# Sums over states turned from channel-by-token to token-by-channel in a bidirectional state-space layer

## The reference, cut to what matters

```
xz = x @ W_in.T
xp, z = split(xz, 2)
xc = silu(conv4(xp) + conv_b)                       # causal, per channel
dt, Bt, Ct = split(xc @ W_xproj.T)
dt = softplus(dt @ W_dt.T + b_dt)
h[t] = exp(dt[t] * A) * h[t-1] + (dt[t] * xc[t]) * Bt[t]    # 16 states per channel
y[t] = sum over states of h[t] * Ct[t]
y = (y + xc * D_param) * silu(z)
out = y @ W_out.T
...
return 0.5 * (mamba(x) + flip(mamba(flip(x))))      # forwards and backwards in time
```

## Time and profile before

| what | value |
|---|---|
| time, median of 3 runs | 4728.89 us (4722.57 to 4737.03) |
| span of the profiled execution, first to last instruction | 4718.1 us |
| POOL busy over the span | 3212.3 us (68%) |
| DVE busy | 3251.1 us (69%) |
| PE busy | 4271.6 us (91%) |
| ACT busy | 2430.7 us (52%) |

### The profile page before, as it was taken

How to read it: one execution, slowest core, us unless ns; L and a number is a source line. 1 busy time by engine, 2 the same in 40 slices (tenths; PEclk the granted TensorE clock), 3 DMA queues, 4 the chain that set the end, 5 groups by cost and what they waited for, 6 DMA issues and landing times. The chain is left out here.

```text
span 4718.1 us, 62490 instructions
## 1 busy us (share of the span) xinstructions
PE 4271.6 (91%) x16896; PEld 2235.4 (47%) x16896; DVE 3251.1 (69%) x5016; ACT 2430.7 (52%) x4880; POOL 3212.3 (68%) x1669
## 2 busy tenths in 40 slices
PE   7999986997899999999999999999999876999994
PEld 4666644664343443344334434433443334666673
DVE  5667773111699999999999999989999975111114
ACT  3555542122566666767676666667666633222221
POOL 3222222442799999999999999999999941444441
PEclk9999996998899999999999999999999987999997
DMA  1000011342334333334333333333333321333456
GB/s 35 21 20 20 20 53 59 108 127 76 107 114 125 115 118 116 121 109 121 122 112 115 112 121 118 116 118 113 117 107 123 114 67 45 110 116 112 127 169 219
DMA packets 267113, 478.79 MB, mean 101 GB/s; under 512 B 39404, under 2 KB 176444, under 8 KB 266908
## 3 DMA queue, kind: packets, MB, share of 16 engines
q1 hardware_dynamic: 235776, 403.02, 26.9%
q0 software_dynamic: 28032, 73.17, 6.1%
q10 hardware_dynamic: 3100, 0.64, 0.1%
HBM read 409.75 MB, written 41.81 MB: 96 GB/s over the span
## 5 line engine op out<-in xcount | busy, mean ns | idle before, releaser
L1804 POOL TENSOR_TENSOR m_xh<-m_u,m_Bb 128x1536 f32<-128x1536 f32 x512 | 1780.1, 3550 | 51.6 <-DVE m_u L1675 39.0
L1731 PE MATMUL bank<-m_xh,ident 128*128 128x512 f32 x3072 | 1455.1, 609 | 34.3 <-POOL m_xh L1793 34.3
L1773 DVE TENSOR_TENSOR_SCAN bank<-bank,m_xh 128x512 f32<-128x512 f32 x864 | 1038.9, 1216 | 44.5 <-ACT bank L1760 42.2
L1760 ACT ACTIVATE bank<-m_dt,m_Ac 128x508 f32<-128x508 f32 x1536 | 1024.9, 683 | 38.4 <-DVE m_xh L1773 38.4
L1731 PEld LDWEIGHTS bank<-m_xh,ident 128*128 128x128 f32 x3072 | 576.2, 194 | 820.0 <-issue 730.7
L1773 DVE TENSOR_TENSOR_SCAN m_xh<-bank,m_xh 128x512 f32<-128x512 f32 x672 | 787.8, 1207 | 64.8 <-ACT bank L1760 59.3
L1793 POOL TENSOR_TENSOR m_xh<-m_xh,m_Cb 128x1536 f32<-128x1536 f32 x224 | 794.0, 3544 | 4.3 <-DVE m_xh L1773 4.0
L1784 DVE TENSOR_TENSOR m_xh<-bank,m_Cb 128x512 f32<-128x512 f32 x864 | 581.3, 673 | 10.9 <-DMA m_Cb<-BC_rows 10.8
L1204 ACT ACTIVATE f1t_h<-bank,f1t_b 128x512 f32<-128x512 f32 (+1 forms) x276 | 147.6, 586 | 509.9 <-PE bank L1234 509.9
L1134 POOL DMA_INDIRECT rows_y<-f1t_y,f1t_home x142 | 139.9, 985 | 316.4 <-DVE f1t_y L1175 287.1
L1579 PE MATMUL bank<-m_xp,m_dg 128*128 128x512 f32 x768 | 351.9, 601 | 3.7 <-DVE m_u L1675 1.4
(11 more groups left out here) (367 smaller groups left out, 6148.3 us busy)
## 6 DMA issues: line engine op xcount, KB each, us to landing
m_Bb<-BC_rows SPq DMA_DIRECT2D x256, 512.0 KB, 4.8
m_Cb<-BC_rows SPq DMA_DIRECT2D x256, 512.0 KB, 4.0
f1t_w<-f_w SPq DMA_DIRECT2D x46, 576.0 KB
m_r<-m_dt POOLq DMA_DIRECT2D x32, 768.0 KB, 7.4
f1t_w1a<-f_w SPq DMA_DIRECT2D x46, 384.0 KB
f0t_w<-f_w SPq DMA_DIRECT2D x22, 576.0 KB
f1c_yg<-rows_y SPq DMA_DIRECT2D x16, 768.0 KB, 8.3
f1t_w1b<-f_w SPq DMA_DIRECT2D x92, 96.0 KB
```

What stands on the lines that cost most here:

```text
L1731: mm = pe.matmul(bank[:, c, :], K.ident[:, :], xh[n % NX][:, c, :], start=False, stop=(d == 1 and n == NS - 1))
L1760: act.activation(o[:, :, lo:hi], seqs(dt[d][:, c, :])[:, :, lo:hi], ACT.Exp, scale=Ac[:, c, n:n + 1]).then_inc(s_dA, 1)
L1773: dve.tensor_tensor_scan(o, bank[:, RING[d][p], way], xh[n % NX][:, c, way], 0.0, ALU.mult, ALU.add).then_inc(s_h, 1)
L1804: pool.tensor_tensor(xh[n % NX][:, :, :], u[d][:, :, :], Bb[q % RB][:, n % QN, :].unsqueeze(1).to_broadcast([P, DC, TOK]), ALU.mult).then_ ...
```

## The change

The sums are kept with tokens on partitions and channels along the free axis. `pe_sum` makes four fp32 transposes of 128 x 128 (one per sequence) that add into PSUM, in place of one product with the identity of 128 x 512. `pe_D` makes four products of 128 columns per block. The gate is computed with tokens on partitions too: four products of 384 columns (`pe_gate`), four copies (`act_gate`). `dve_y` becomes four multiplications of 128 x 384, and each needs all three blocks' sums. Since W_out still wants channels on partitions, the gated rows are turned back: for each block c four transposes on PE (`pe_yT`) into bank `NB` and a copy by ACT (`act_ys`) into `lw`, which `pe_out` then reads. The D terms of a group now all follow the last `dve_y` of the group before, at units 13 to 15; a sum may catch up three units at a time instead of two. `pe_out` moves from units 17 and 18 to 18 and 20, `dve_out` from 14 and 15 to 16 and 17, `pe_dt1` from 20 to 22 up to 22 to 24.

```diff
-            "y": (6, 7, 9), "pe_D0": (14, 15, 17), "pe_D1": (6, 16, 25), "pe_out": (17, 18), "out": (14, 15),
+            "y": (6, 7, 8, 9), "pe_D0": (13, 14, 15), "pe_D1": (6, 16, 25), "pe_yT": (15, 16, 17), "act_ys": (15, 16, 17),
+            "pe_out": (18, 20), "out": (16, 17),
...
-        ys = r
+        ysT = r.rearrange("p c t -> p (c t)").rearrange("p (s x) -> p s x", s=G)
...
-        gz = sb("gz", [P, DC, TOK])
+        ys = lw
+        gz = sb("gz", [P, G, DC * P])
+        yb = bank[:, 0:DC, :].rearrange("p b x -> p (b x)")
...
-                m = slice((DC + c) * P, (DC + c + 1) * P)
-                pe.matmul(bank[:, front(c), :], win_a[:, m], zTa[:, :], start=True, stop=False)
-                pe.matmul(bank[:, front(c), :], win_b[:, m], zTb, start=False, stop=True).then_inc(s_zps, 1)
+                m, t = slice(DC * P, 2 * DC * P), slice(c * P, (c + 1) * P)
+                pe.matmul(bank[:, NB, 0:DC * P], zTa[:, t], win_a[:, m], start=True, stop=False)
+                pe.matmul(bank[:, NB, 0:DC * P], zTb[:, t], win_b[:, m], start=False, stop=True).then_inc(s_zps, 1)
...
         def pe_D(pe, g, d, c):
             pe.wait_ge(s_xc, g * 2 + d + 1)
-            if d == 0 and later(g):
-                pe.wait_ge(s_gy, (g - 1) * DC + c + 1)
+            if d == 0 and c == 0 and later(g):
+                pe.wait_ge(s_gy, g * G)
...
-            pe.matmul(bank[:, c, :], dgD[:, c, :], xc[d][:, c, :], start=(d == 0), stop=False).then_inc(s_D, 1)
+            for i in range(G):
+                b = i * DC + c
+                mm = pe.matmul(yb[:, b * P:(b + 1) * P], xc[d][:, c, i * P:(i + 1) * P], dgD[:, c, :],
+                               start=(d == 0 and c == 0 and i != 1), stop=False, skip_group_check=True)
+            mm.then_inc(s_D, 1)
...
-            mm = pe.matmul(bank[:, c, :], K.ident[:, :], xh[n % NX][:, c, :], start=False, stop=(d == 1 and n == NS - 1))
+            for i in range(G):
+                b = i * DC + c
+                mm = pe.matmul(yb[:, b * P:(b + 1) * P], xh[n % NX][:, c, i * P:(i + 1) * P], K.ident[:, :], is_transpose=True,
+                               start=False, stop=(d == 1 and n == NS - 1), skip_group_check=True)
             mm.then_inc(s_red, 1)
+
+        def pe_yT(pe, g, c):
+            if c == 0:
+                pe.wait_ge(s_gy, g * G + G)
+                if not (isinstance(g, int) and g == NG - 1):
+                    pe.wait_ge(s_pj, g * 2 + 4)
+                    stand_alone(pe, K.go)
+            else:
+                pe.wait_ge(s_ys, g * DC + c)
+            for i in range(G):
+                mm = pe.transpose(bank[:, NB, i * P:(i + 1) * P], ysT[:, i, c * P:(c + 1) * P], K.ident[:, :])
+            mm.then_inc(s_ysps, 1)
+
+        def act_ys(act, g, c):
+            act.wait_ge(s_ysps, g * DC + c + 1)
+            if c == 0:
+                act.wait_ge(s_spps, (g + 1) * 2 * DC + (DC if not (isinstance(g, int) and g == NG - 1) else 0))
+            act.copy(ys[:, c, :], bank[:, NB, :]).then_inc(s_ys, 1)
 
         def pe_out(pe, g, i):
             if i == 0:
-                pe.wait_ge(s_gy, g * DC + DC)
-                if not (isinstance(g, int) and g == NG - 1):
-                    pe.wait_ge(s_pj, g * 2 + 4)
+                pe.wait_ge(s_ys, g * DC + DC)
...
-        def dve_y(dve, g, c):
-            dve.wait_ge(s_red, (g * 2 * NS + 2 * NS - 1) * DC + c + 1)
-            if c == 0:
+        def dve_y(dve, g, i):
+            if i == 0:
+                dve.wait_ge(s_red, (g + 1) * 2 * NS * DC)
                 dve.wait_ge(s_gz, g + 1)
-            dve.tensor_tensor(ys[:, c, :], bank[:, c, :], gz[:, c, :], ALU.mult).then_inc(s_gy, 1)
+            dve.tensor_tensor(ysT[:, i, :], yb[:, i * DC * P:(i + 1) * DC * P], gz[:, i, :], ALU.mult).then_inc(s_gy, 1)
...
-                now = list(range(done, min(upto, done + 2)))
+                now = list(range(done, min(upto, done + 3)))
```

More of the change, by code:

```diff
@@ L1434, in mamba_phase @@
         s_er, = ctx.software(K, 1)
-        s_gy, s_ops, s_out = sem("gated_ready"), sem("outps_ready"), sem("res_ready")
+        s_gy, s_ysps, s_ys = sem("gated_ready"), sem("gated_back"), sem("gated_copied")
+        s_ops, s_out = sem("outps_ready"), sem("res_ready")
         def seqs(t):
@@ L1558, in pe_gate @@
                 else:
-                    pe.wait_ge(s_zc, g * DC + c)
-                m = slice((DC + c) * P, (DC + c + 1) * P)
-                pe.matmul(bank[:, front(c), :], win_a[:, m], zTa[:, :], start=True, stop=False)
-                pe.matmul(bank[:, front(c), :], win_b[:, m], zTb, start=False, stop=True).then_inc(s_zps, 1)
+                    pe.wait_ge(s_zc, g * G + c)
+                m, t = slice(DC * P, 2 * DC * P), slice(c * P, (c + 1) * P)
+                pe.matmul(bank[:, NB, 0:DC * P], zTa[:, t], win_a[:, m], start=True, stop=False)
+                pe.matmul(bank[:, NB, 0:DC * P], zTb[:, t], win_b[:, m], start=False, stop=True).then_inc(s_zps, 1)
             def act_gate(act, c):
-                act.wait_ge(s_zps, g * DC + c + 1)
+                act.wait_ge(s_zps, g * G + c + 1)
                 if c == 0 and deep:
-                    act.wait_ge(s_gy, g * DC)
-                act.copy(gz[:, c, :], bank[:, front(c), :]).then_inc(s_zc, 1)
+                    act.wait_ge(s_gy, g * G)
+                act.copy(gz[:, c, :], bank[:, NB, 0:DC * P]).then_inc(s_zc, 1)
             def pe_conv(pe, c):
@@ L1643, in act_ln @@
                     act.wait_ge(s_spps, s * DC)
+                if d == 1 and deep:
+                    act.wait_ge(s_ops, g * 2)
                 act.activation(lw[:, :, :], w1[d][:, :, :], ACT.Ln).then_inc(s_ln, 1)
@@ L1656, in pe_sp @@
                     if d == 1:
-                        pe.wait_ge(s_zc, g * DC + DC)
+                        pe.wait_ge(s_zc, g * G + G)
                         stand_alone(pe, K.go)
@@ L1695, in chain @@
                     continue
-                for c in range(DC):
+                for c in range(G if name == "gate" else DC):
                     put("pe", POS[f"pe_{name}{d}"][c], on_pe, c)
@@ L1719, in pe_D @@
             pe.wait_ge(s_xc, g * 2 + d + 1)
-            if d == 0 and later(g):
-                pe.wait_ge(s_gy, (g - 1) * DC + c + 1)
-            elif d == 0:
+            if d == 0 and c == 0 and later(g):
+                pe.wait_ge(s_gy, g * G)
+            elif d == 0 and c == 0:
                 pe.wait_ge(s_u, DC)
-            pe.matmul(bank[:, c, :], dgD[:, c, :], xc[d][:, c, :], start=(d == 0), stop=False).then_inc(s_D, 1)
+            for i in range(G):
[3 more added lines that the diff above has]
+            mm.then_inc(s_D, 1)
         def pe_sum(pe, g, d, n, c):
@@ L1855, in sums_at @@
                 upto = p + 1 - LAG * DC
-                begun = sum(p >= at for at in POS["pe_D0"])
-                if carry and begun < DC:
-                    upto = min(upto, begun)
-                now = list(range(done, min(upto, done + 2)))
+                if carry and p < POS["pe_D0"][-1]:
+                    upto = min(upto, 0)
+                now = list(range(done, min(upto, done + 3)))
                 plan.append(now)
@@ L1909, in main @@
                             pe_sum(pe, *at_step(g, d, k // DC), k % DC)
+                    if carry and p in POS["pe_yT"]:
+                        pe_yT(pe, g - 1, POS["pe_yT"].index(p))
                     if carry and p in POS["pe_out"]:
@@ L1916, in after @@
                             pe_sum(pe, NG - 1, 1, n, c)
+                    for c in range(DC):
+                        pe_yT(pe, NG - 1, c)
                     for i in two:
@@ L1924, in main, with after @@
                     act_decay(act, g, d, p)
-                program(act, "act", main, lambda act: None, lambda act: None)
+                    if d == 0 and later(g) and p in POS["act_ys"]:
+                        act_ys(act, g - 1, POS["act_ys"].index(p))
+                def after(act):
+                    for c in range(DC):
+                        act_ys(act, NG - 1, c)
+                program(act, "act", main, lambda act: None, after)
             @block.gpsimd
@@ L1956, in after @@
                     dve_read(dve, NG - 1, 1, UNITS - 1)
-                    for c in range(DC):
-                        dve_y(dve, NG - 1, c)
+                    for i in range(G):
+                        dve_y(dve, NG - 1, i)
                     for i in two:
```

8 lines of the change are left out of this document (4 added, 4 removed), and 4 rows, old and new, of the table POS.

## The result

The changed kernel takes 4899.36 us, median of 4 runs (4897.85 to 4906.4), the kernel before 4728.53 beside it: a ratio of 1.0367 (95% interval 1.035 to 1.0383). It is slower by 171 us, outside the range of the prediction. The profiled execution has a span of 4896.1 us.

A forecast was written before the change was run, and what follows sets the result against it. POOL was taken to bound the state-space layer (159.94 of 162.96 us a group). Terms -29 + 20 + 2 = -7 us on a span of 4718.1 gave about 4711, a 4722 us median (own range 4708 to 4738); overall range 4700 to 4762.

The forecast's parts named there:

- the 36.3 us: POOL's waits in the layer for u inside the loop, sum slots and DVE's scans: all a faster PE can win.
- PE's freed 38 us a group: PE time saved by shorter sums, taken to cover the extra D and gate products, which were costed at nothing.
- The slower rival: Clock falls ahead of the second convolution block as PE idles; gate 2.4 us later, +36, 4758 us; chance 0.18.
- one sign that the text gave: Clock at 0.50 around the second convolution block, with scan waits at state 3, would show the clock was the cause.
- The rule that spoke against it: Skill page: transposes don't count as busy TensorE, so sums as transposes would not hold the clock; 4758 us by it.
- The new wait: DVE waits 2.9 and 1.1 us at the output additions; POOL feels 1.3 us a group, +20 us.
- the faster rival: The turning back is hidden, POOL feels 0.3 us a group: -26, 4703 us; chance 0.28.
- The 1.0 us gained at the gate: DVE's wait for sums at the first gate multiplication, 1.95 us, gets 1.0 us shorter, between 0 and 1.6.
- The gain of 29 us: Shorter sums cut POOL's waits: 16 us for u, 10 for slots, 3 for scans; bounds -36 and -12.
- Sums: A sum on PE becomes four fp32 transposes, 0.46 us in place of 0.855, saving 38 us a group.
- an accumulating transpose costs a product's time: Rival: sums stay at 0.855 us, nothing of the gain is won, the new wait stays: +22, 4751 us; chance 0.09.
- The end: After the last sum nothing hides the turn: gate to first output 7.9 us, today 4.7; +2 us in all.

The follow-up runs named there:

- e9_fill_first: The changed kernel with products of zeros filling TensorE's waits in the chain of a group's first half alone, none for the second half: 4751.1 us.
- e1_plain: The changed kernel with its sums as ordinary fp32 products by the identity instead of transposes, all else as changed: 5048.4 us.
- e4_before_late: The kernel before with only the changed kernel's later positions for output, dt products, gate and softplus steps; sums and layout as before: 4800.1 us.
- e11_noturn_fill: The changed kernel with waits filled by products of zeros, no turning back, output products at 12 and 15, other chain steps at the old positions: 4742.1 us.
- e10_sched2_fill: The changed kernel with waits filled by products of zeros, and turning back, output products and additions, dt products and softplus steps moved earlier: 4791.8 us.
- e6_fill: The changed kernel with products of a tile of zeros filling TensorE's waits in both halves of a group, order and positions as changed: 4755.1 us.

## Why the prediction was wrong

**The step that failed** is the one that priced PE's freed time at nothing: "PE isn't the bound, so the gain is the part of the 36.3 us that was due to it", and behind it "PE's freed 38 us a group covers them". The sum priced every product on the chain at the full clock. The freed time became waits of PE, and the clock fell for the products that u depends on. Filling the waits of the first half, and nothing else, takes 4899.4 to 4751.1: 148 of the 171 us.

**The slower rival had the mechanism and too small a size.** It named a clock that falls because shorter sums leave PE idle, but put it at one block of the second convolution (36 us, chance 0.18). A fall does stand there: PE waits 5.31 us for ACT, the clock is at 0.53, and the block takes 5.23 us where it took 3.61. PE's block, its window, and POOL's read of state 3:

```profile
1562.10 5.23 PE L1583 MATMUL bank<-m_xp,m_dg 128*128 128x512 f32 x8 [5.31 <-ACT m_xc L1591]
...
1561.58:1565.00 3.42, 2.90 (x4) 1.34 (x5) 3.42 (x4) 2.53 (x6) 3.42 (x2) 0.53 0.21 53
...
1583.47 3.44 POOL L1822 TENSOR_TENSOR m_xh<-m_xh,m_Cb 128x1536 f32<-128x1536 f32 x1 [0.74 <-DVE m_xh L1802]
```

But the block lost 1.6 us and not 3.4, and POOL waits only 0.74 us at state 3, where it waited up to 0.4 before. The clock is low for 45 us a group, and what counts are the dt, gate and softplus products of the first half, behind which POOL waits at states 10 and 12. So one sign that the text gave (the clock around this block) was seen, the other (waits at state 3) hardly.

**The rule that spoke against it.** By the Trainium skill, "TensorE: Matmul & The Clock Gate", Part 4, transposes would not hold the clock. With the waits filled by transposes the clock was 0.96, by products 0.98, by nothing 0.87. So transposes held it nearly as well as products; the measurement decides against the rule for this case.

**The new wait** was right in its mechanism, and the faster rival with its hidden turn fell: 2.97 and 1.30 us at `dve_out` for 2.9 and 1.1. DVE reaches unit 18 at T0 + 10.4 (1598.18, with T0 at the end of the second row addition, 1587.79), for T0 + 10. The 1.0 us gained at the gate didn't come: DVE waits 1.85 us there, before 1.95, and 1.71 with the clock held (e9_fill_first). What POOL feels was mis-sized: with the clock held 2.5 us a group, not 1.3, some 18 us over 15 groups.

**The gain of 29 us** is there, all but a few us, once the clock is held. In e9_fill_first POOL waits for u only at the layer's start, so all of the 19.8 us inside the loop are won (forecast 16), and 7.1 of the 12.5 for sums (forecast 10); the 41.2 us for scans, 37 more than before, are the new wait (forecast 20). In the changed kernel the gain is buried: the wait for sums, forecast to vanish, rose to 38.8 us.

**Sums** take 0.109 us a record, start to start, 0.46 in all, as forecast; that an accumulating transpose costs a product's time is refuted. By e1_plain the change would have cost 320 us with long sums, the stop at the loop's turn included. PE's busy share of the layer fell from 0.97 to 0.81, by a sixth and not by a quarter.

**The end** was mis-sized: from the last group's first gating to its first output 11.6 us (3986.69 to 3998.31), for 4.7 before and 7.9 forecast, at a clock of 0.57. That is 3.7 us over the forecast; the wait ahead of the gating fell from 2.77 to 1.41 us, about as forecast.

What stays open: why each fall comes where it does. Some follow one wait of 3 us or more, that of the dt products only waits under 1 us. In e4_before_late PE did the same in the 7 us ahead of the third dt product in both groups shown (busy 6.70 us, one wait of 0.30), and the clock fell in one and not in the other. So the fillings show that more work on PE holds the clock, not that a wait alone lowers it; whether the dt products, with 12 rows of 128, have a part in it was not tested. Open is also how much of e11_noturn_fill's missing gain is its own order.

## What to carry to other kernels

Time saved on TensorE in a kernel that it doesn't bound isn't free: if it turns into short waits, the granted clock can fall, and products that others wait for take up to twice as long (2.07 us for 1.12 here). Look at the granted clock over the stage before and after, and price each product on the critical chain at both levels. Where the chain matters more than the work, cheap products in the waits can be worth more than the saving itself (148 us here, for a saving forecast at 29); and steps placed by hand should be moved with the engine's order in mind, since a wait that an engine reaches too early in its order (ACT's 5.84 us in e10_sched2_fill) costs as well as one that comes too late.

## What the hardware showed that was not expected

The granted clock went to 0.51 for 10.2 us behind a stretch in which PE was busy 5.41 of 6.60 us and no wait was longer than 0.85 us. In e4_before_late, with long sums, it went to 0.50 behind a stretch in which PE was busy 6.70 of 7.00 us, in every second group alone. Some 45 us a group at the lower level cost 10 us of time, nearly all in the first half; in the second half e9_fill_first stood (0.98 - 0.95)/0.5 of 164 us, 10 us a group, longer at the lower level than e6_fill and lost nothing. Transposes of zeros held the clock nearly as well as bf16 products of zeros (0.96 and 0.98). PE stopped at the loop's turn with 11,961 records in 14 groups (52.4 us in 13 turns) and with 13,949 (42.9 us), and in no run with 10,267 or fewer.
